# Cross attention batch by batch, with four of seven row units turned by VectorE through DRAM

## The reference, cut to what matters

```python
# 32 batches of 56 rows x 256; a context of 32 x 1500 x 128; masks all true
q = (x @ Wq).reshape(B, 56, 16, 128); k = ctx @ Wk; v = ctx @ Wv      # 16 heads, 8 key heads
scores = einsum('bhtd,bhsd->bhts', q, k) / sqrt(128)
attn = softmax(where(mask, scores, -inf))
y = einsum('bhts,bhsd->bhtd', attn, v).reshape(B, 56, 2048) @ Wo
# before it: self attention with a layernorm; behind it: a layernorm and a mixture of experts
```

## Time and profile before

| what | value |
|---|---|
| time, median of 3 runs | 1717.78 us (1717.73 to 1717.91) |
| the profiled execution, span | 1718.6 us |
| TensorE busy, of the span | 98% |
| VectorE, ScalarE, GpSimd busy | 71%, 55%, 39% |
| bytes moved by DMA | 140.29 MB |
| a pair of batches in the middle | 82 us |

### The profile page before, as it was taken

One profiled execution on the slowest core, in us unless ns is written; L12 is line 12 of the kernel. 1 busy time (PEld: TensorE's weight loads), 2 busy tenths in 40 slices (PEclk: granted clock), 3 DMA queues, 4 the chain that ended last, 5 costly groups with the idle time before them and its releaser, 6 DMA issues.

```text
span 1718.6 us, 28903 instructions
## 1 busy us (share of the span) xinstructions
PE 1685.0 (98%) x10034; PEld 1517.0 (88%) x10034; DVE 1221.3 (71%) x3377; ACT 937.2 (55%) x1717; POOL 664.6 (39%) x417
## 2 busy tenths in 40 slices
PE   7999999999999999999999999999999999999996
PEld 7998889898989898989898989989898989888985
DVE  5655676877787878777778777776878787756557
ACT  5444465656565656565656565565656565644543
POOL 1220344525243333333334343443525341355435
PEclk9999999999999999999999999999999999999998
DMA  5234643423141423333232323232324130431433
GB/s 197 81 132 130 193 95 78 70 68 81 54 97 41 90 44 88 48 86 68 62 68 63 68 63 68 70 66 77 74 61 89 52 57 12 112 114 40 121 90 95
DMA packets 102856, 140.29 MB, mean 82 GB/s; under 512 B 37022, under 2 KB 81728, under 8 KB 102592
## 3 DMA queue, kind: packets, MB, share of 16 engines
q1 hardware_dynamic: 60784, 115.47, 26.8%
q10 hardware_dynamic: 38912, 14.80, 4.0%
q0 software_dynamic: 3024, 8.26, 1.8%
HBM read 113.62 MB, written 24.89 MB: 81 GB/s over the span
## 4 chain that ended last, share of the span: by engine, by line
PE 93%; DVE 2%; issue 1%; ACT 1%; DMA 1%; POOL 0%; another core or an unknown queue 0%; POOLq 0%; SPq 0%; ACTq 0%; DVEq 0%
PE b_turn L831 17%; PE b_out L850 9%; PE b_out L851 9%; PE b_out L852 9%; PE b_score L817 9%; PE b_score L819 9%; PE b_score L818 9%; PE b_out L860 5%; PE a_bank L344 5%; PE c_gate L1513 2%; PE c_down L1540 1%; PE a_bank L370 1%; PE a_bank L395 1%; PE a_bank L424 1%; PE a_bank L417 1%
## 5 line engine op out<-in xcount | busy, mean ns | idle before, releaser
L895 ACT CAST b_pT_hi<-b_turn 125x512 fp32r<-125x512 f32 (+1 forms) x768 | 406.8, 530 | 543.0 <-PE b_turn L831 539.8
L997 DVE TENSOR_TENSOR b_pT_lo<-b_turn,b_pT_hi 125x512 fp32r<-125x512 f32 (+1 forms) x768 | 478.0, 623 | 259.7 <-ACT b_pT_hi L895 254.2
L983 DVE CUSTOM_DVE_ANT_0 b_p<-b_score,b_mask_add 128x500 f32<-128x500 f32 x672 | 451.9, 673 | 58.9 <-PE b_turn L831 24.4
L831 PEld LDWEIGHTS b_turn<-ident,b_p 128*125 128x125 f32 x2688 | 409.4, 186 | 55.2
L831 PE MATMUL b_turn<-ident,b_p 128*125 128x128 f32 x2688 | 418.1, 272 | 0.0
L901 ACT ACTIVATE b_p<-b_p,b_shift 128x1500 f32<-128x1500 f32 x224 | 347.5, 1551 | 2.1 <-DVE b_top_min L991 2.1
L850 PE MATMUL b_out<-b_pT_hi,b_c_hi 125*128 125x512 f32 (+1 forms) x768 | 346.5, 451 | 0.7 <-DVE b_pT_lo L997 0.6
L1135 POOL TENSOR_TENSOR b_oT_lo<-b_oT,b_oT_hi 128x896 fp32r<-128x896 f32 x32 | 67.6, 2112 | 624.5 <-ACT b_oT_hi L925 588.0
L851 PE MATMUL b_out<-b_pT_lo,b_c_hi 125*128 125x512 f32 (+1 forms) x768 | 280.9, 366 | 0.0
L852 PE MATMUL b_out<-b_pT_hi,b_c_lo 125*128 125x512 f32 (+1 forms) x768 | 280.5, 365 | 0.0
L817 PE MATMUL b_score<-b_cT_hi,b_q_hi 128*128 128x500 f32 x672 | 262.9, 391 | 0.0
(11 more groups left out here) (250 smaller groups left out, 2402.1 us busy)
## 6 DMA issues: line engine op xcount, KB each, us to landing
cT_in<-in_ctxT SPq DMA_DIRECT2D x32, 750.0 KB, 9.8
b_c_in<-in_ctx SPq DMA_DIRECT2D x32, 750.0 KB
q_store<-a_fold_in_or_q_stage SPq DMA_DIRECT2D x16, 896.0 KB, 4.2
q_in<-q_store SPq DMA_DIRECT2D x32, 448.0 KB, 7.1
b_rden_all<-rden_store ACTq DMA_DIRECT2D x32, 256.0 KB, 3.6
b_rden_all<-rden_store ACTq DMA_DIRECT2D x32, 192.0 KB, 3.7
b_mask_in<-in_mask SPq DMA_DIRECT2D x32, 187.5 KB, 9.4
slot_store<-c_y2T SPq DMA_DIRECT2D x35, 128.0 KB, 1.7
```

What stands on the lines that cost most here:

```text
L831: mm = pe.transpose(turn_bank[n % 3][0:CK, u * 128:(u + 1) * 128], p[slot % 2][:, u, c * CK:(c + 1) * CK], ident[:])
L895: act.copy(pT_hi[:, n % 3, 0:w], turn_bank[n % 3][0:CK, 0:w]).then_inc(hi_done, 1)
L983: dve.tensor_tensor_reduce(out=p[slot % 2][:, u, keys], in0=score_bank[j][:, 0:FW], in1=mask_add[:, b, keys], scale=1.0, scalar=-3.0e38, o ...
L997: dve.tensor_tensor(pT_lo[:, n % 3, 0:w], turn_bank[n % 3][0:CK, 0:w], pT_hi[:, n % 3, 0:w].bitcast(F32), ALU.subtract).then_inc(lo_done, 1)
```

## The change

The cross attention goes by batches of 24 steps. The fills of the seven units are spread over the 24 steps. The three units of the odd part stay as they were: turned by TensorE at steps 2 to 13 of the next batch, weighed at steps 4 to 15. The four units of the even part are no longer turned by TensorE. VectorE turns each whole unit in 32 x 32 blocks with one instruction (`turn_blocks`, L1090) into `by_block`, which SP stores to a DRAM tensor `p_store`, 768 KB a unit. When all four are stored and the batch ahead is weighed, SP loads them back with the keys on the partitions into `keyed`: 16 transfers of 192 KB for a batch (`load_keyed`, L803), whose DRAM side is written as 4 x 32 x 384 numbers and whose SBUF side as 128 x 384. ScalarE rounds chunks of `keyed` to `pT_hi` (L968); the rest is subtracted in place by GpSimd for two of three chunks (L1244) and by VectorE for the third (L1101), in the last batch for all. TensorE weighs them at steps 16 to 27, counted from the start of the next batch.

With it: ScalarE instead of GpSimd rounds `cT` and `c`; the projection is cut in four pieces; `keyed` is a single buffer of 24 KB a partition, and buffers elsewhere are laid over each other to make room; the last phase gets its weights in another order.

```diff
+        keyed = sb("keyed", [128, EVEN * QUADS, ACROSS])
+        keyed_lo = written_over("keyed", [128, EVEN * QUADS, ACROSS], F32R)
...
+        HI_AT = STEPS + 2
+        PV_AT = HI_AT + 2
+        BLOCKS_AT = (5, 9, 13, 17)
...
+            def load_c(m):
+                if m >= 2:
+                    sp.wait_ge(pv_done, whole(m - 2))
+                sp.dma_start(c_raw[m % 2][:], D["ctx"][m]).then_inc(c_loaded[m % 2], 16)
+
+            def store_p(m, u):
+                sp.wait_ge(blocks_turned, EVEN * m + u + 1)
+                if m >= 2:
+                    sp.wait_ge(keyed_loaded, 16 * QUADS * EVEN * (m - 1))
+                sp.dma_start(D["p"][m % 2, u].rearrange("q a n -> q (a n)"),
+                             by_block[:].rearrange("q al b j -> q (al b j)")).then_inc(p_stored, 16)
+
+            def load_keyed(m, u):
...
+                if m:
+                    sp.wait_ge(pv_done, whole(m - 1))
+                sp.wait_ge(p_stored, 16 * EVEN * (m + 1))
+                for a in range(QUADS):
+                    sp.dma_start(keyed[:, QUADS * u + a, :],
+                                 D["p"][m % 2, u, 32 * a:32 * (a + 1)].rearrange("i al n -> al i n")).then_inc(keyed_loaded, 16)
...
+            for m in range(B):
+                if m >= 2:
+                    load_c(m)
+                if m:
+                    store_p(m, 0)
+                    for u in range(EVEN):
+                        load_keyed(m - 1, u)
+                if m + 2 < B:
+                    load_q(m + 2)
+                if m:
+                    store_p(m, 1)
+                store_p(m, 2)
...
+            def weigh_even(m, c):
...
+                if m < LAST and c % 3 < 2:
+                    pe.wait_ge(keyed_lo_done[0], 2 * (CH // 3) * m + c - c // 3 + 1)
+                else:
+                    pe.wait_ge(keyed_lo_done[1], CH // 3 * m + (c if m == LAST else c // 3) + 1)
...
+            def keyed_round(m, c):
+
+                if c == 0:
+                    act.wait_ge(keyed_loaded, 16 * QUADS * EVEN * (m + 1))
+                act.wait_ge(pv_done, STEPS * m + CH + c - 2)
+                act.copy(by_blocks(pT_hi[:, c % 3, :]), keyed_chunk(keyed, c)).then_inc(hi_done, 1)
...
+            def turn_blocks(m, u):
+
+
+                dve.wait_ge(exp_done, PUNITS * m + u + 1)
+                dve.wait_ge(p_stored, 16 * (EVEN * m + u))
+                own = row(m, u)
+                keys = bass.AP(own.tensor, own.offset, [own.ap[0], [32, QUADS], [CK, CH], [1, 32]])
+                dve.transpose(by_block[:], keys).then_inc(blocks_turned, 1)
...
             def p_rest(m, c):
+                w = 128 * ODD
```

More of the change, by code:

```diff
@@ L726, in lagging @@
[L726 to L744, removed]
-            return None
@@ L747, in sync, with fill_step @@
-        def sync(sp):
[L748 to L766, removed]
+        def fill_step(f):
+            return f * (PUNITS + 1) // PUNITS
@@ new lines, in fills_at, with unit_ends, parity, behind @@
+        def fills_at(n):
+            return [f for f in range(PFILLS) if fill_step(f) == n]
+        def unit_ends(n, late):
+            return [f // FILLS for f in range(FILLS - 1, PFILLS, FILLS) if fill_step(f) + late == n]
+        def parity(u):
+            return (0, u) if u < EVEN else (1, u - EVEN)
+        def behind(m, n, at, count=1):
+            for k in range(3):
+                if at <= n + STEPS * k < at + count and 0 <= m - k:
+                    return m - k, n + STEPS * k - at
+            return None
@@ new lines, in units_behind, with row, whole, keyed_chunk @@
+        def units_behind(m, n, late, last):
+            ends = [] if last else [(m, u) for u in unit_ends(n, late)]
+            return ends + ([(m - 1, u) for u in unit_ends(n + STEPS, late)] if m else [])
+        def row(m, u):
+            return p[0][:, (EVEN * m + u) % EVEN_DEEP, :] if u < EVEN else p[1][:, u - EVEN, :]
+        def whole(m):
+            return STEPS * (m + 1)
+        def keyed_chunk(tensor, c):
+            return tensor[0:CK, :, 32 * c:32 * (c + 1)]
+        def by_blocks(ap):
+            return ap.rearrange("p (g j) -> p g j", j=32)
@@ L776, in load_ahead @@
             def load_ahead():
[L777 to L793, removed]
-                residual(i - 1)
-                load_values(i, 1)
@@ L797, in sync @@
-            loads(1, first=True)
-            with sp.Fori(2, NPAIR) as i:
-                loads(i)
-            store(NPAIR - 2)
-            residual(NPAIR - 1)
+                load_mask(0)
+                load_c(0)
+            store_last_part, wait_stored = opening.sync(sp, load_ahead)
+            load_q(1)
+            load_cT(1)
+            load_mask(1)
+            load_c(1)
+            for part in range(len(opening.stored)):
+                if part >= 2:
+                    store_p(0, part - 2)
+                store_last_part(part)
@@ new lines, in gpsimd @@
+            mask_bias(0)
+            pool.wait_ge(*opening.queried)
+            for m in range(B):
+                if m >= 2:
+                    oT_rest(m - 2)
+                if m < LAST:
+                    split_q(m + 1)
+                    cT_rest(m + 1)
+                    mask_bias(m + 1)
+                c_rest(m)
+                if m:
+                    for c in range(CH):
+                        keyed_rest(m - 1, c)
+                        if c == 1 and m % 2 and m >= 3:
+                            rstd((m - 3) // 2)
@@ L1224, in phase_c @@
         count_r = queries.take("c_count_r", [1, RP])
-        places_2, tiles_2 = odd.again(), odd.again()
+        ones, half = queries.take("c_ones", [128, 128]), queries.take("c_half", [128, 1])
+        turned_p.at = edge["p1"] - 2 * 4 * H_DEEP * 512
         h_hi = turned_p.take("c_h_hi", [128, H_DEEP, 512], F32R)
@@ L2059, in _ @@
             tokens_of_tiles()
[L2060 removed]
+            for s in range(X_FIRST):
                 fetch_x(s)
```

732 lines of the change are left out of this document (394 added, 338 removed).

## The result

The changed kernel takes 2718.67 us, the median of 4 runs (2716.22 to 2725.63), against 1717.76: a ratio of 1.583, 95% interval 1.581 to 1.585. That is 129 us above the predicted 2590 and inside the range. One of the four executions of e9, a variant further down, took 2534.16 us at a granted clock of 0.556; its time and ratio there are of the other three.

A forecast was written before the change was run, and what follows sets the result against it. TensorE, 98% busy, bounded the kernel before; afterwards a transfer loop on four DMA engines would, at 68.4 us a batch. Rest 407 + first batch 92 + thirty loops 2052 + last 47 - 8 = 2590 us, range 2010 to 2770 (0.8).

The forecast's parts named there:

- term 1: Start of each batch's loop, from the end of step 3: the context's load goes first, on five engines, 9.0 us.
- term 3: The 16 loads of keyed in each batch, on four DMA engines: 33.6 us, and 1.0 for the last to land.
- rivals with all 16 engines: Loads of keyed on 16 engines: loop still late, 1750 us, chance 0.05; or all hidden, 1596 us, chance 0.10.
- the 42.1 us a batch of the first: Rival: loads of keyed on all 16 engines, loop still closes late; 42.1 us a batch, 1750 us in all, chance 0.05.
- terms 2 and 3: Behind the context's load: store of unit 0, 1.9 us, then the 16 loads, 33.6 us, and 1.0 to land.
- term 4: After the loads: ScalarE rounds chunk 0 of keyed, GpSimd subtracts, two hand-overs; 2.2 us.
- terms 5 to 7: Loop's end: TensorE's steps 16 to 27, 17.0 us; VectorE's hold, 2.0; TensorE's restart at half clock, 1.7.
- The hold: VectorE's turn of unit 2 waits for unit 1's store, queued behind the 16 loads: 2.0 us a batch (0 to 6).
- Half clock: TensorE, after idling some 28 us in each batch, restarts at half clock: 1.7 us.
- The signs: Expected in the trace: DMA share near 0.25, ScalarE's wait for keyed longest, TensorE near 60% busy, batch every 68 us.
- The ends: Outside the thirty loops: first batch 92 us, last batch 47, less 8 of the opening's work falling into the first.
- the rival's 1596 us: Rival: loads on all 16 engines, all hidden, TensorE's own 36.7 us is the batch; 1596 us, chance 0.10.

The follow-up runs named there:

- e9: e8 with two buffers for the block turn instead of one, and even-part scores two units deep instead of three: 1760.07 us, ratio 1.024.
- e4: Changed kernel with the reciprocals stored in runs of 12 or 16 bytes instead of 4-byte pieces, in another order: 2571.92 us, ratio 1.498.
- e5: Changed kernel with the context's load cut in two, of 112 and 13 rows: 2636.87 us, ratio 1.534.
- e11: Changed kernel with two buffers for the block turn instead of one, and the same shorter scores as e9: 2629.95 us, ratio 1.530.
- e1: Changed kernel with the same 16 loads of keyed cut to an outermost count of 32 on both sides: 2197.87 us, ratio 1.281.
- e6: Changed kernel with the edits of e1 and e4 together: 2008.43 us, ratio 1.169.
- e2: Changed kernel with each load of keyed cut in two, 32 loads with an outermost count of 2 on the DRAM side: 3709.29 us, one run.
- e12: e9 with the loads of keyed ahead of the store of the next batch's first unit on SP's queue: 1692.82 us, ratio 0.986.
- e7: e6 with the context's load also cut in 112 and 13 rows, as in e5: 1982.45 us, ratio 1.154.
- e8: Changed kernel with e4, e5 and blocks sorted when storing: four stores of 32 partitions and one load a unit: 1923.97 us, ratio 1.120.
- e13: e12 with the reciprocals stored as in the changed kernel, in 4-byte pieces, so it computes all of the reference: 1909.36 us, ratio 1.111.

## Why the prediction came out as it did

The loop in the prediction's own stretches, in us from the issue of the context's load on; the runs are means over the 29 batches from batch 2's to batch 31's load:

| to | forecast | changed | e4 | e5 | e11 | e1 | e6 |
|---|---|---|---|---|---|---|---|
| ScalarE's rounding of the context (term 1) | 9.0 | 14.6 | 9.8 | 12.0 | 14.7 | 17.8 | 9.9 |
| its first rounding from `keyed` (2, 3) | 36.5 | 33.5 | 33.9 | 33.5 | 33.6 | 14.0 | 16.4 |
| the first weighing from `keyed` (4) | 2.2 | 2.1 | 2.1 | 2.1 | 2.1 | 2.1 | 2.1 |
| the next context load (5 to 7) | 20.7 | 20.8 | 20.7 | 20.8 | 18.4 | 21.1 | 20.6 |
| batch | 68.4 | 71.0 | 66.5 | 68.4 | 68.7 | 55.0 | 49.0 |

- **Four engines for the loads (term 3).** Right: a share of 0.27 at 100 GB/s, against 0.25 at 95 forecast. e1 and e2 move the time as the outermost count says. The rivals with all 16 engines fall by the trace; and e1 shows that the 42.1 us a batch of the first was too low as well: with 16 engines and nothing else altered it is 55.0. In e6, without the small pieces, it is still 49.0: the stretch of the loads is 16.4, where that rival had 9 + 1.9 + 1.0.
- **Context and store ahead (terms 1 and 2).** The term that was mis-sized is the context's load: 14.6 us, forecast 9.0. The stretch behind it is 3.0 shorter than terms 2 and 3 made it, as the store of unit 0 lies beside the context (180 GB/s from 1309 to 1312, where the context alone moved 111 to 127). So two errors stand against each other, and that the batch came within 2.6 us of the sum is in part luck. The cause of the first is the 4-byte pieces, which the prediction named only at the upper end of its range, among things that "get in the way": e4 takes them out and the stretch is 9.8. It fits that the 9.0 came from a load of before that was issued 10 us behind such a store (829.25); in the change it is issued 2.4 us behind one (1303.53). The two stores, before and after:

```profile
818.83 0.38 ACTq L908 DMA_DIRECT2D rden_store<-b_rden  x1
```

```profile
1301.13 0.38 ACTq L982 DMA_DIRECT2D rden_store<-b_rden  x1
```

The prediction also didn't see that ScalarE waits for the context before it does the odd part's roundings.
- **Hand-overs (term 4).** 2.1, forecast 2.2.
- **Steps 16 to 27 with hold and clock (terms 5 to 7).** 20.8, forecast 20.7. The hold, 2.0 of it, measures 2.4 in this stretch and 2.25 in the batch by e11. Half clock is seen in the stretches (0.50 from 1352 to 1356, 1.00 at 1360); no run took it away, so its 1.7 is not measured by itself.
- **The block turn**: 1.77 us, forecast 1.7.
- **The signs.** One of them fails: ScalarE's wait for `keyed`, 22.4 us a time, is not the longest. VectorE's for `p_store` is longer in all (844.4 against 694.6 us), and that it stands so long costs only the 2.25 us that e11 shows.
- **The ends.** Of the 129 us missed, some 76 are in the loops (309.37 to 2436.99 where 30 loops made 2052). The last batch holds some 20: from the end of its step 3 to the first weighing from `keyed` the sum has 33.6 + 1 + 2.2 = 36.8 us, the trace 56.4. SP is held by the loads, and what stands behind them comes late:

```profile
2436.99 30.98 SPq L803 DMA_DIRECT2D b_keyed<-p_store  x16
...
2478.30 1.46 SPq L1466 DMA_DIRECT2D c_y<-y_store  x3
```

```profile
2485.92 1.12 PE L1532 MATMUL c_turn<-ident,c_y 128*128 128x128 f32 x4 [37.68 <-DMA c_y<-y_store]
...
2493.38 0.50 PE L916 MATMUL b_out<-b_pT_hi,b_c_hi 125*128 125x512 f32 x1 [1.22 <-DVE b_keyed_over L1101]
```

TensorE, in order, waits 37.7 us for the last phase's input (`c_y`) with the odd part's steps queued behind them. The remaining 33 us lie in the first two batches:

```profile
223.83 1.78 DVE L1090 STREAM_TRANSPOSE b_by_block<-b_p 128x1536 f32<-128x1536 f32 x1 [13.67 <-DMA p_store<-b_by_block]
```

```profile
233.12 3.35 POOL L1226 TENSOR_TENSOR b_cT_lo<-cT_in,b_cT_hi 128x1500 fp32r<-128x1500 f32 x1 [25.75 <-ACT b_cT_hi L1003]
```

```profile
236.57 0.76 PE L865 MATMUL b_score<-b_cT_hi,b_q_hi 128*128 128x500 f32 x1 [7.46 <-issue]
```

VectorE waits 13.7 us for the single buffer at the first batch's fourth turn, for which the sum had nothing; e11, where that wait is gone, starts its loop 18 us earlier. Another 7.5 are TensorE's wait until the second batch's `cT` is rounded, which e11 has too (7.6). The rest, some 7, stays open.
- **What the change saves.** In the best variant, e12, TensorE is busy for 37.9 of 40 us, so for 37.0 in a batch of 39.0: the forecast 36.7 for its own work stands. The work was saved, but of the 138 to 172 us forecast for it e12 shows 25, and the rival's 1596 us was reached by no variant.

Open: whether the reciprocals can be stored in the right order and in longer pieces, which would make e12's time that of a full kernel. That wasn't tried. Nor were the same pieces stored at a time when no load stands behind them, a second buffer for `keyed`, or a load of half the bytes on the same four engines.

## What to carry to other kernels

Before work is moved from an engine to DMA, write down both sides of each transfer as counts and look for the largest number up to 16 that divides both outermost ones: here it was four, and SP was held for 34.0 us, where e1's cut held it for 16.1 and e7's for 9.3. Then look at what else is in flight where the transfer will stand, tiny pieces above all, and at what waits behind it on its queue. The cut itself was worth 521 us here. The pieces, the context's five engines, the rows sorted on the way out, the second buffer of the block turn and the order on SP's queue were worth 505 together (e1 to e12). Of these, two buffers on the storing side gave 164 us (e8 to e9), and the transfer that closes the loop, put first on its queue, gave 67 (e9 to e12).

## What the runs showed of the hardware that I had not expected

- A queue whose transfers use few engines holds its issuer: 16 issues take SP 34.0 us on four engines, and on 16 engines 16.1 in e1 and 9.3 in e7. The same bytes as four loads of 768 KB take it 2.2 us in e12.
- Behind a store of 384 or 512 pieces of 4 bytes the context's load moves 20 GB/s for 6 us in the changed kernel (at a DMA share of 0.17), and 25 and 37 GB/s in the 8 us of e13 (at 0.89 and 0.69). In the kernel before, landings beside them fall from 8.0 to 5.3 us (`cT`) and from 9.9 to 4.3 (mask) when they become 128 runs of 12 or 16 bytes.
- A store of 768 KB to DRAM needs a median of 9.9 us to land beside this traffic, where the bytes alone are 2.3 at 342 GB/s.
- VectorE turns 128 x 1536 float32 in 32 x 32 blocks in 1.77 us, less than three times the 0.69 of a subtraction of 512.
